# A conditioned transformer block on one core: the feed-forward's square sums made one slot earlier and turned behind x in the gate's bank

## The chip, the cores and the metric

The kernel runs on one core of one Trainium2 chip. The metric is device time in microseconds (us) of one execution. The kernel before takes 960.4 us, the median of three runs (960.19 to 960.7).

The engines named below: PE is TensorE (matrix products and transposes into PSUM), DVE is VectorE, ACT is ScalarE, POOL is GpSimd, and SP (SyncE) issues the transfers. Each engine executes its own list of instructions in order, and lists meet only through semaphores.

## The reference, cut to what matters

The input is 128 sequences of 64 tokens of 256 features, with one condition vector of 64 numbers for each sequence. All is float32.

```
x = layernorm(x) * weight + bias + tanh(cond @ lin_w.T + lin_b);  x = x * weight + bias
x = x + a_alpha * attention(a_gamma * rms(x) + a_beta)          # 16 heads of 16, softmax over 64 keys
x = x + f_alpha * ((silu(h @ gate_w.T) * (h @ hidden_w.T)) @ out_w.T + out_b),  h = f_gamma * rms(x) + f_beta
rms(x) = x / sqrt(mean(x * x over the 256 features) + 1e-6)
```

The gammas, betas and alphas are products of the condition with small matrices, one vector of 256 per sequence. The hidden width is 1024.

## The kernel before, in words

**Parts, slots, groups.** The 8192 tokens are worked in 32 parts of 256 tokens (four sequences). Features lie on the partitions and tokens along them, in two halves (KT = 2). One loop over slots `s`, from -8 to 141, is written out on every engine with the same conditions. A slot holds one sequence's attention (two, in every second slot) and one step of the feed-forward, whose four steps for a part fill one group of four slots. With `grp, j = s // 4, s % 4`, a group does at the same time: the first normalisation of part `grp + 2`, the keys, queries and values of part `grp + 1`, scores and softmax of part `grp`, attention's output of part `grp - 1` (at j = 3), the second normalisation of part `grp - 2`, and the feed-forward steps (gate, hidden, down) of part `grp - 3`. Below, "first slot" is j = 0 and "fourth slot" j = 3.

**Precision.** Each float32 product is made in three passes over rounded operands of type fp32r: an operand is split into `_hi` and `_lo` (ACT rounds to `_hi`, DVE or POOL subtracts to make `_lo`), and `three_pass` multiplies hi by hi, hi by lo and lo by hi (L361 to L363). Such a product, with 256 columns, is the bulk of what PE does.

**The second normalisation of part m = grp - 2.** Attention's output lies in bank 7 (`work`); DVE multiplies it by alpha (`gate_attention`, L777, writes `gated_a`), POOL adds it to the residual (`add_attention`, L1275), both in the fourth slot of the group before. In the first slot ACT squares the residual (`square_f`, L990) and POOL adds the two halves (`sum_squares_f`, L1223). In the second slot PE turns the 128x256 sums into PSUM in two transposes (`turn_squares`, L408), so that DVE can add over the features along a row (`mean_squares_out`, L785 and L788); POOL raises the result to -1/2 (`inverse_rms`, L1203). In the third slot PE spreads the inverse back over the partitions (`spread_inverses`, L415), DVE scales by it (L791), POOL adds beta; in the fourth, ACT and DVE split (`split_hi_f` L1002, `ffn_split_lo` L812, which writes `xf_lo`). The feed-forward of that part begins in the first slot of the next group.

**PSUM banks around this.** The gate's products go to bank 0, the hidden ones to bank 1, the output's to bank 2. Bank 1 is also `norm_bank`: in it x is turned (`turn_x`, L396, first slot), the square sums are turned (second slot) and the inverses are spread (third slot), each between two uses of it by `hidden`. So `turn_squares` waits in the second slot for `prod_made` of the step before. Bank 0 is also where the probabilities of every odd sequence are turned (L521), to be copied out by ACT (`probs_out`, L1055) before the gate's products of the same slot are begun. ACT takes tanh of the gate's bank (L1070), DVE multiplies it with the same bank (`activate`, L819) and with the hidden bank (`product`, L827), ACT rounds (L1076), DVE subtracts (`product_lo`, L833).

**DVE's list in a first slot**: `product_lo` of the step before (L833), a tiny instruction on token statistics (L716), the two minima of this slot's scores (`find_least`, L743, one for each of two sequences), and then the softmax's sums. For parts from 6 on, DVE also shifts the tokens of x, one tile of 128 at a time (`shift_tokens`, L703 and L707, writes `xin`), or takes their statistics (L669, then the small merges from L676). In the slot ahead of an even group a tile is shifted; in the slot ahead of an odd group the statistics are merged.

## Time and profile before

| | |
|---|---|
| median of 3 runs | 960.4 us (960.19 to 960.7) |
| profiled execution | 959.94 us, of which the span of instructions 958.1 us |
| granted TensorE clock | 0.999 |
| PE busy | 919.5 us, 96% of the span |
| DVE busy | 740.5 us, 77% |
| ACT busy | 634.9 us, 66% |
| POOL busy | 501.0 us, 52% |

The profile gives, for one execution, each engine's busy time, the time at which each instruction starts and how long it takes, and what an engine waited for. Two records of one engine that follow each other overlap a little: on DVE the next one starts some 0.08 us before the last one's end, and PE starts a new 256-column product every 0.12 us though its record is 0.28 us long. So a row's start time is what to compare with another row's start time.

### The profile page before, as it was taken

The page shows a single profiled execution, that of the slowest core. Times are in us where ns is not written, and L with a number is a line of the kernel's source. Part 1 is how long each engine was busy: PE and PEld are TensorE (multiplying, and loading weights), DVE is VectorE, ACT ScalarE, POOL GpSimd, SP SyncE. Part 2 cuts the span into 40 slices and gives each one's busy share as a digit, 9 for nine tenths or more (in the row PEclk, how much of TensorE's full clock was granted, in tenths as well). Part 3 has the DMA queues.
Part 4 walks back from the last instruction along what each step waited for, and adds up shares of the span by engine and source line. Part 5 has one row for each costly group of instructions (what it writes and reads, how often), then busy time and mean ns, then how long its engine had stood idle before and what let it go on. Part 6 is the DMA issues. An engine that isn't in the chain of part 4 may idle for free.

```text
span 958.1 us, 28583 instructions
## 1 busy us (share of the span) xinstructions
PE 919.5 (96%) x11064; PEld 883.9 (92%) x11064; DVE 740.5 (77%) x1433; ACT 634.9 (66%) x1837; POOL 501.0 (52%) x479
## 2 busy tenths in 40 slices
PE   5667999999999999999999999999999999999997
PEld 4557999999999999999999999999999999998997
DVE  5977788788778778877877887887788787667654
ACT  3656766767776776777677677767667766766432
POOL 4686455465655555555455555545555555453320
PEclk9999999999999999999999999999999999999999
DMA  6200011120020212002121210202110110100000
GB/s 224 75 2 29 13 24 56 25 51 22 10 57 24 57 24 51 13 18 57 23 57 24 49 12 20 58 24 56 25 36 23 24 36 18 18 13 13 13 12 24
DMA packets 40631, 33.77 MB, mean 35 GB/s; under 512 B 10800, under 2 KB 39984, under 8 KB 40496
## 3 DMA queue, kind: packets, MB, share of 16 engines
q1 hardware_dynamic: 40496, 31.93, 13.3%
q8 instruction: 89, 1.46, 0.7%
q14 instruction: 46, 0.38, 0.3%
HBM read 23.37 MB, written 8.55 MB: 33 GB/s over the span
## 4 chain that ended last, share of the span: by engine, by line
PE 89%; DVE 5%; issue 3%; POOL 2%; ACT 1%; DMA 0%; SPq 0%; DVEq 0%; ACTq 0%; POOLq 0%
PE psum L361 18%; PE psum L363 18%; PE psum L362 18%; PE psum L587 6%; PE psum L589 6%; PE psum L588 6%; PE psum L521 5%; PE psum L495 4%; PE psum L537 4%; PE psum L396 2%; PE psum L415 1%; DVE least L743 1%; PE psum L408 1%; POOL probs L1270 0%; DVE row_sum L759 0%
## 5 line engine op out<-in xcount | busy, mean ns | idle before, releaser
L361 PE MATMUL psum<-xf_hi,ffn_hi 128*128 128x256 f32 x1024 | 291.3, 284 | 2.1 <-ACT probsT L1055 1.6
L362 PE MATMUL psum<-xf_lo,ffn_hi 128*128 128x256 f32 x1024 | 288.1, 281 | 0.0
L363 PE MATMUL psum<-xf_hi,ffn_lo 128*128 128x256 f32 x1024 | 287.8, 281 | 0.0
L1047 ACT ACTIVATE probs<-psum,least 128x64 f32<-128x64 f32 x928 | 204.5, 354 | 38.5 <-DVE least L743 37.7
L1270 POOL TENSOR_TENSOR probs<-probs,inv_sum 128x512 f32<-128x512 f32 x128 | 133.9, 1047 | 154.1 <-DVE inv_sum L764 154.0
L361 PEld LDWEIGHTS psum<-xf_hi,ffn_hi 128*128 128x128 f32 x1024 | 192.7, 188 | 3.2 <-issue 2.7
L362 PEld LDWEIGHTS psum<-xf_lo,ffn_hi 128*128 128x128 f32 x1024 | 192.8, 188 | 0.0
L363 PEld LDWEIGHTS psum<-xf_hi,ffn_lo 128*128 128x128 f32 x1024 | 192.8, 188 | 0.0
L1076 ACT ACTIVATE prod_hi<-late 128x512 fp32r<-128x512 f32 x128 | 83.3, 651 | 127.6 <-DVE late L827 127.5
L587 PE MATMUL psum<-prod_hi,ffn_hi 128*128 128x256 f32 x512 | 144.1, 281 | 0.9 <-DVE prod_lo L833 0.9
L589 PE MATMUL psum<-prod_hi,ffn_lo 128*128 128x256 f32 x512 | 144.1, 282 | 0.0
L588 PE MATMUL psum<-prod_lo,ffn_hi 128*128 128x256 f32 x512 | 144.1, 281 | 0.0
L759 DVE TENSOR_REDUCE row_sum<-probs 128x8 f32<-128x512 f32 x128 | 87.0, 680 | 71.6 <-ACT probs L1047 71.6
L819 DVE SCALAR_TENSOR_TENSOR late<-tanh,psum 128x512 f32<-128x512 f32 x128 | 87.2, 681 | 64.6 <-ACT tanh L1070 63.4
L1070 ACT ACTIVATE tanh<-psum 128x512 f32<-128x512 f32 x128 | 78.3, 612 | 49.0 <-PE psum L363 46.6
L833 DVE TENSOR_TENSOR prod_lo<-late,prod_hi 128x512 fp32r<-128x512 f32 x128 | 93.4, 730 | 20.4 <-ACT prod_hi L1076 20.2
L1055 ACT ACTIVATE probsT<-psum 128x512 f32<-128x512 f32 x128 | 69.4, 594 | 54.9 <-PE psum L537 54.9
L587 PEld LDWEIGHTS psum<-prod_hi,ffn_hi 128*128 128x128 f32 x512 | 96.4, 188 | 1.1 <-issue 1.1
L1256 POOL TENSOR_TENSOR normed_f<-normed_f,mod 128x512 f32<-128x512 f32 x32 | 33.4, 1043 | 120.7 <-DVE normed_f L791 120.7
L589 PEld LDWEIGHTS psum<-prod_hi,ffn_lo 128*128 128x128 f32 x512 | 96.4, 188 | 0.0
L588 PEld LDWEIGHTS psum<-prod_lo,ffn_hi 128*128 128x128 f32 x512 | 96.4, 188 | 0.0
L743 DVE TENSOR_REDUCE least<-psum 128x8 f32<-128x512 f32 x128 | 82.7, 684 | 16.2 <-PE psum L495 16.2
(116 smaller groups left out, 2154.4 us busy)
## 6 DMA issues: line engine op xcount, KB each, us to landing
out_t_dram<-x_res SPq DMA_DIRECT2D x31, 256.0 KB, 3.0
xin<-x_dram SPq DMA_DIRECT2D x15, 512.0 KB, 6.7
shift_tok<-shift_rows SPq DMA_DIRECT2D x104, 64.0 KB, 3.1
inv_row<-inv_rows SPq DMA_DIRECT2D x26, 128.0 KB, 4.8
w_raw<-attn_w_dram SPq DMA_DIRECT2D x1, 1024.0 KB, 6.7
x_res<-gate_w_dram SPq DMA_DIRECT2D x1, 1024.0 KB, 9.4
late<-hidden_w_dram SPq DMA_DIRECT2D x1, 1024.0 KB, 11.3
w_raw<-out_w_dram SPq DMA_DIRECT2D x1, 1024.0 KB, 6.4
```

The source lines that it names most:

```text
L361: pe.matmul(out, stat_hi, mov_hi, start=first, stop=False)
L362: pe.matmul(out, stat_hi, mov_lo, start=False, stop=False)
L363: return pe.matmul(out, stat_lo, mov_hi, start=False, stop=last)
L587: pe.matmul(out, ffn_hi[:, 2, cols], hi, start=q == 0 and mt == 0 and u == 0, stop=False)
L588: pe.matmul(out, ffn_hi[:, 2, cols], prod_lo[f % 2][:, tok], start=False, stop=False)
L589: mm = pe.matmul(out, ffn_lo[:, 2, cols], hi, start=False, stop=q == 3 and mt == KT - 1 and u == 1)
L743: dve.tensor_reduce(least[g % 2][:].rearrange("p (r a) -> p r a", r=4), scores[g % 2], AX_X, ALU.min).then_inc(least_made, 1)
L759: dve.tensor_reduce(row_sum[g % 2][:], probs[g % 4][:].rearrange("p (h k) -> p h k", k=SEQ), AX_X, ALU.add).then_inc(sum_made, 1)
L819: dve.scalar_tensor_tensor(out=act_gate, in0=tanh[:], scalar=1.0, in1=gate_bank, op0=ALU.add, op1=ALU.mult).then_inc(act_made, 1)
L833: dve.tensor_tensor(prod_lo[f % 2][:], prod, prod_hi[f % 2][:].bitcast(F32), ALU.subtract).then_inc(prod_lo_made, 1)
L1047: op = act.activation(probs[g % 4][:, h * SEQ:(h + 1) * SEQ], scores[g % 2][:, h // 2, h % 2], ACT.Exp, bias=least[g % 2][:, h:h + 1], sca ...
L1270: pool.tensor_tensor(by_head, by_head, inv_sum[g % 2][:].unsqueeze(2).broadcast_to([P, 8, SEQ]), ALU.mult).then_inc(probs_made, 1)
```

## The change

Three things are done, for parts 2 to 31 (`sums_ahead`).

1. Attention's output is added first in the fourth slot: DVE's `gate_attention` moves ahead of `product_lo`, and POOL's `add_attention` moves ahead of `normalise_probs` (multiplying the probabilities) and `split_lo_a` (`xn_lo`).
2. The square sums are made in that same fourth slot: ACT squares after its tanh, ahead of rounding the product, and POOL adds the halves last in the slot.
3. The sums are turned in the next first slot, right behind x's four transposes, and into the gate's bank instead of bank 1. For this PE waits until the gate's bank has been read by `activate` and by the copy of the probabilities. DVE reads the sums right after the two minima, and the first gate product of the group waits until they are read (`ms_read`). In the second slot nothing of it is left.

No instruction is added or taken away.

```
+        def sums_ahead(m):
+            return 2 <= m < NPART
+
+        def square_bank(grp):
+            return gate_bank if sums_ahead(grp - 2) else norm_bank
...
             def gate(f):
...
+                if f % PSEQ == 0 and sums_ahead((f + FFN_AT) // PSEQ - 2):
+                    pe.wait_ge(ms_read, (f + FFN_AT) // PSEQ + 3)
...
         # PE's list
                     norm_bank_free(s)
                     if j == 0 and is_part(grp + 2):
                         turn_x(grp + 2)
+                if j == 0 and sums_ahead(grp - 2):
+                    pe.wait_ge(act_made, min(f, FFN_STEPS))
+                    if is_seq(s - 1):
+                        pe.wait_ge(probsT_out, s)
+                    turn_squares(grp)
...
-                if j == 1 and is_group(grp) and s >= 0:
+                if j == 1 and is_group(grp) and s >= 0 and not sums_ahead(grp - 2):
                     norm_bank_free(s)
                     turn_squares(grp)
...
         # DVE's list
-                if j == 1 and is_group(grp):
+                if j == 1 and is_group(grp) and not sums_ahead(grp - 2):
                     mean_squares_out(grp)
+                if j == 3 and sums_ahead(grp - 1):
+                    gate_attention(grp - 1)
                 if is_step(f - 1):
                     product_lo(f - 1)
...
+                if j == 0 and sums_ahead(grp - 2):
+                    mean_squares_out(grp)
...
         # ACT's list
-                if j == 0 and is_part(grp - 2) and s > FFN_AT:
-                    square_f(grp - 2)
...
                 if is_step(f):
                     half_tanh(f)
+                if j == 3 and sums_ahead(grp - 1):
+                    square_f(grp - 1)
...
         # POOL's list
+                if j == 3 and sums_ahead(grp - 1):
+                    add_attention(grp - 1)
                 if is_seq(s) and not wide(s):
                     normalise_probs(s)
...
-                if j == 3 and is_part(grp - 1):
+                if j == 3 and is_part(grp - 1) and not sums_ahead(grp - 1):
                     add_attention(grp - 1)
+                if j == 3 and sums_ahead(grp - 1):
+                    sum_squares_f(grp - 1)
```

The lists show it. In all of them the line numbers of the changed kernel are a few higher than those of the kernel before for the same code, and what stands in brackets are the semaphores that the instruction waits for.

PE, before, in a first slot, from the scores to the keys:

```order
L495 MATMUL psum<-k_heads,q_heads 64x128 x15
L396 MATMUL psum<-ident,xin 128x128 [waits y_tok,prod_made]
L396 MATMUL psum<-ident,xin 128x128 x3
L361 MATMUL psum<-xn_hi,w_hi 128x256 [waits gated_a_made,lo_a,probsT_out]
L362 MATMUL psum<-xn_lo,w_hi 128x256
```

PE, changed, at the same place (`xf_hi` begins the gate's products, after twelve of the keys, of which the rows between are left out):

```order
L501 MATMUL psum<-k_heads,q_heads 64x128 x15
L402 MATMUL psum<-ident,xin 128x128 [waits y_tok,prod_made]
L402 MATMUL psum<-ident,xin 128x128 x3
L414 MATMUL psum<-ident,square_sum_f 128x128 [waits sq_sum_f,probsT_out,act_made]
L414 MATMUL psum<-ident,square_sum_f 128x128
L367 MATMUL psum<-xn_hi,w_hi 128x256 [waits gated_a_made,lo_a,probsT_out]
...
L367 MATMUL psum<-xf_hi,ffn_hi 128x256 [waits ms_read,probsT_out,act_made,lo_f]
```

The two transposes of the sums now stand between x and the keys, and the gate's first product has `ms_read` as a further wait.

DVE, before, from the fourth slot of an odd group into the first slot of the next one:

```order
L833 TENSOR_TENSOR prod_lo<-late,prod_hi 128x512 [waits out_mm,prod_hi_made]
...
L777 TENSOR_TENSOR gated_a<-psum,mod 128x512 [waits resid_made,wo_mm]
L819 SCALAR_TENSOR_TENSOR late<-tanh,psum 128x512 [waits prod_made,tanh_made]
...
L812 TENSOR_TENSOR xf_lo<-normed_f,xf_hi 128x512 [waits hi_f]
L703 SCALAR_TENSOR_TENSOR xin<-xin,mean,rows 128x256
L707 SCALAR_TENSOR_TENSOR xin<-xin,rstd,shift_tok 128x256 [waits shift_loaded0,centred]
L833 TENSOR_TENSOR prod_lo<-late,prod_hi 128x512 [waits out_mm,prod_hi_made]
L716 TENSOR_SCALAR token_inv<-token_ms 128x2 [waits inv_sent,sq_tok]
L743 TENSOR_REDUCE least<-psum 128x8 [waits scores_read,scored] x2
L759 TENSOR_REDUCE row_sum<-probs 128x8 [waits scores_read]
```

DVE, changed, at the same place:

```order
L790 TENSOR_TENSOR gated_a<-psum,mod 128x512 [waits resid_made,wo_mm]
L846 TENSOR_TENSOR prod_lo<-late,prod_hi 128x512 [waits out_mm,prod_hi_made]
...
L825 TENSOR_TENSOR xf_lo<-normed_f,xf_hi 128x512 [waits hi_f]
L716 SCALAR_TENSOR_TENSOR xin<-xin,mean,rows 128x256
L720 SCALAR_TENSOR_TENSOR xin<-xin,rstd,shift_tok 128x256 [waits shift_loaded0,centred]
L846 TENSOR_TENSOR prod_lo<-late,prod_hi 128x512 [waits out_mm,prod_hi_made]
L729 TENSOR_SCALAR token_inv<-token_ms 128x2 [waits inv_sent,sq_tok]
L756 TENSOR_REDUCE least<-psum 128x8 [waits scores_read,scored] x2
L798 TENSOR_REDUCE square_mean<-psum 128x2 [waits inv_spread,ms_mm]
L801 TENSOR_SCALAR mean_sq<-square_mean 128x2 [waits ms_read]
L772 TENSOR_REDUCE row_sum<-probs 128x8 [waits scores_read]
```

(`xf_lo` is the lower half of the feed-forward's input, `xin` the tile of x that is being shifted.) `gated_a` has moved ahead of `prod_lo`, and the sums (`square_mean`, `mean_sq`) now follow the two minima.

POOL, before, over the same stretch:

```order
L1270 TENSOR_TENSOR probs<-probs,inv_sum 128x512 [waits inv_sum_made] x2
L1243 TENSOR_TENSOR xn_lo<-normed_a,xn_hi 128x512 [waits hi_a]
L1275 TENSOR_TENSOR x_res<-x_res,gated_a 128x2x256 [waits gated_a_made]
L1210 TENSOR_TENSOR token_inv<-token_inv,minus_half 128x2 [waits token_ms_out]
L1223 TENSOR_TENSOR square_sum_f<-squares_f 128x256 [waits ms_mm,squared_f]
L1251 TENSOR_TENSOR normed_f<-x_res,mod 128x512 [waits lo_f,resid_made]
```

POOL, changed:

```order
L1287 TENSOR_TENSOR probs<-probs,inv_sum 128x512 [waits inv_sum_made]
L1292 TENSOR_TENSOR x_res<-x_res,gated_a 128x2x256 [waits gated_a_made]
L1287 TENSOR_TENSOR probs<-probs,inv_sum 128x512 [waits inv_sum_made]
L1260 TENSOR_TENSOR xn_lo<-normed_a,xn_hi 128x512 [waits hi_a]
L1240 TENSOR_TENSOR square_sum_f<-squares_f 128x256 [waits ms_mm,squared_f]
L1227 TENSOR_TENSOR token_inv<-token_inv,minus_half 128x2 [waits token_ms_out]
L1268 TENSOR_TENSOR normed_f<-x_res,mod 128x512 [waits lo_f,resid_made]
```

The addition to `x_res` now comes first and the square sums last of the fourth slot, with the product of the probabilities and `xn_lo` between them.

## Rows read from the trace of the kernel before

**Rows 1.** Windows, steady stretch: window, length, busy us per engine, clock, DMA, GB/s.
```profile
120.00:840.00 720.00, 720.00 (x8800) 697.29 (x8799) 574.27 (x1103) 508.37 (x1529) 391.08 (x370) 1.00 0.15 33
```

**Rows 2.** Timeline of PE, probabilities turned in an even group's first slot: start us, us.
```profile
503.25 1.03 PE L521 MATMUL psum<-ident,probs 128*128 128x128 f32 x8
```

**Rows 3.** Timeline of PE, first slot of an even group, from the scores on.
```profile
504.80 0.69 PE L495 MATMUL psum<-k_heads,q_heads 32*64 32x128 f32 x32
505.42 0.66 PE L396 MATMUL psum<-ident,xin 128*128 128x128 f32 x4
505.84 0.37 PE L361 MATMUL psum<-xn_hi,w_hi 128*128 128x256 f32 x1
...
507.35 0.28 PE L361 MATMUL psum<-xf_hi,ffn_hi 128*128 128x256 f32 x1
```

**Rows 4.** Timeline of DVE, fourth slot into that first slot.
```profile
499.64 0.69 DVE L833 TENSOR_TENSOR prod_lo<-late,prod_hi 128x512 fp32r<-128x512 f32 x1
...
501.08 0.65 DVE L777 TENSOR_TENSOR gated_a<-psum,mod 128x512 f32<-128x512 f32 x1
...
502.55 0.69 DVE L827 TENSOR_TENSOR late<-psum,late 128x512 f32<-128x512 f32 x1
503.15 0.93 DVE L812 TENSOR_TENSOR xf_lo<-normed_f,xf_hi 128x512 fp32r<-128x512 f32 x1
504.00 1.50 DVE L703 SCALAR_TENSOR_TENSOR xin<-xin,mean,rows 128x256 f32<-128x256 f32 x1
...
506.61 1.28 DVE L743 TENSOR_REDUCE least<-psum 128x8 f32<-128x512 f32 x2
```

**Rows 5.** Timeline of POOL, the same stretch.
```profile
501.25 1.04 POOL L1270 TENSOR_TENSOR probs<-probs,inv_sum 128x512 f32<-128x512 f32 x1 [3.85 <-DVE inv_sum L764]
502.25 1.28 POOL L1243 TENSOR_TENSOR xn_lo<-normed_a,xn_hi 128x512 fp32r<-128x512 f32 x1
503.50 1.72 POOL L1275 TENSOR_TENSOR x_res<-x_res,gated_a 128x512 f32<-128x512 f32 x1
...
507.46 0.73 POOL L1223 TENSOR_TENSOR square_sum_f<-squares_f 128x256 f32<-128x256 f32 x1
```

**Rows 6.** Timeline of ACT, the copies of the probabilities there.
```profile
504.77 1.09 ACT L1055 ACTIVATE probsT<-psum 128x512 f32<-128x512 f32 x2 [0.87 <-PE psum L537]
```

**Rows 7.** Timeline of DVE, the sums' read in the second slot.
```profile
513.79 0.41 DVE L785 TENSOR_REDUCE square_mean<-psum 128x2 f32<-128x256 f32 x1
```

**Rows 8.** Timeline of PE, the last products of the span.
```profile
952.50 0.36 PE L587 MATMUL psum<-prod_hi,ffn_hi 128*128 128x256 f32 x1 [0.90 <-DVE prod_lo L833]
```

**Rows 9.** Timeline of DVE, what releases them.
```profile
951.66 0.69 DVE L833 TENSOR_TENSOR prod_lo<-late,prod_hi 128x512 fp32r<-128x512 f32 x1 [0.70 <-ACT prod_hi L1076]
```

**Rows 10.** Timeline of DVE, first slot of an odd group.
```profile
534.57 1.28 DVE L743 TENSOR_REDUCE least<-psum 128x8 f32<-128x512 f32 x2
```

**Rows 11.** Timeline of PE, the gate's first product there.
```profile
535.47 0.28 PE L361 MATMUL psum<-xf_hi,ffn_hi 128*128 128x256 f32 x1
```

**Rows 12.** Timeline of PE, second slot: the sums' transposes and what follows.
```profile
513.04 0.38 PE L408 MATMUL psum<-ident,square_sum_f 128*128 128x128 f32 x2
513.18 0.37 PE L361 MATMUL psum<-xf_hi,ffn_hi 128*128 128x256 f32 x1
513.38 0.28 PE L362 MATMUL psum<-xf_lo,ffn_hi 128*128 128x256 f32 x1
```

**Rows 13.** Timeline of DVE, first slot of group 4.
```profile
113.06 1.28 DVE L743 TENSOR_REDUCE least<-psum 128x8 f32<-128x512 f32 x2
```

**Rows 14.** Timeline of PE, the gate's first product there.
```profile
112.81 0.28 PE L361 MATMUL psum<-xf_hi,ffn_hi 128*128 128x256 f32 x1
```

**Rows 15.** Timeline of DVE, first slot of group 31.
```profile
870.57 1.29 DVE L743 TENSOR_REDUCE least<-psum 128x8 f32<-128x512 f32 x2 [1.01 <-PE psum L495]
```

**Rows 16.** Timeline of PE, gate's first products, groups 31 and 32; bracket: idle before.
```profile
870.97 0.36 PE L361 MATMUL psum<-xf_hi,ffn_hi 128*128 128x256 f32 x1 [0.51 <-ACT probsT L1055]
...
896.21 0.36 PE L361 MATMUL psum<-xf_hi,ffn_hi 128*128 128x256 f32 x1 [1.13 <-ACT probsT L1055]
```

More of the change, by code:

```diff
@@ L403, in turn_squares @@
                     for i in range(2):
-                        mm = pe.transpose(norm_bank[:, i * P:(i + 1) * P], square_sum_a[:, i * P:(i + 1) * P], ident[:])
+                        mm = pe.transpose(square_bank(grp)[:, i * P:(i + 1) * P], square_sum_a[:, i * P:(i + 1) * P], ident[:])
                 if is_part(grp - 2):
@@ L407, in turn_squares @@
                     for i in range(2):
-                        mm = pe.transpose(norm_bank[:, (2 + i) * P:(3 + i) * P], square_sum_f[:, i * P:(i + 1) * P], ident[:])
+                        mm = pe.transpose(square_bank(grp)[:, (2 + i) * P:(3 + i) * P], square_sum_f[:, i * P:(i + 1) * P], ident[:])
                 mm.then_inc(ms_mm, 1)
@@ L784, in mean_squares_out @@
                 cols = norm_cols(grp, 1)
-                dve.tensor_reduce(square_mean[:, cols], norm_bank.rearrange("p (n c) -> p n c", c=P)[:, cols], AX_X, ALU.add
+                dve.tensor_reduce(square_mean[:, cols], square_bank(grp).rearrange("p (n c) -> p n c", c=P)[:, cols], AX_X, ALU.add
                                   ).then_inc(ms_read, 1)
@@ L1311, in _ @@
                 if j == 0 and is_part(grp - 2) and not wide(s):
-                    sum_squares_f(grp - 2)
+                    if not sums_ahead(grp - 2):
+                        sum_squares_f(grp - 2)
                     apply_gamma_f(grp - 2)
@@ L1331, in _ @@
                     split_lo_a(grp + 2)
-                if j == 3 and is_part(grp - 1):
+                if j == 3 and is_part(grp - 1) and not sums_ahead(grp - 1):
                     add_attention(grp - 1)
+                if j == 3 and sums_ahead(grp - 1):
+                    sum_squares_f(grp - 1)
                 if j == (grp == 1) and grp % 2 == 1 and 1 <= (grp + 3) // 2 < NBLK:
```

## The prediction

> **What bounds the kernel now.** I read the page's busy times first, where PE is far ahead of the others. Then the windows: over the 720 us from 120 to 840 PE is busy for all 720.00, at full clock (column 1.00), and DVE for 574 [rows 1]. Whatever PE idles lies at the two ends. So in the steady stretch nothing that another engine saves can pay; only PE's own list can become shorter, and any new wait on it comes out in full. The question is therefore what the change makes PE wait for. For that I read the timelines of the four engines around one first slot, and ask for each of the waits added to PE when its releaser would be ready. The steady groups are alike in two kinds, even (a tile of x is shifted in the slot ahead) and odd (statistics are merged there); one of each is read.
>
> **PE's list.** In the second slot the two transposes and their surroundings go. The transposes start at 513.04 and the second product behind them at 513.38, 0.34 us, where a product alone takes 0.12; so PE saves 0.22 us for each group [rows 12]. In the first slot x's four transposes take 505.84 - 505.42 = 0.42 us, 0.105 each [rows 3]; two more in the same chain cost 0.21. By itself the move is worth nothing: the same two transposes, elsewhere.
>
> **The new waits in front of the transposes** are three. `act_made` lies before `prod_made`, which x's transposes wait for already: nothing. `probsT_out`: the second copy ends at 504.77 + 1.09 = 505.86 [rows 6], while x's transposes are through at 505.84 [rows 3]: about 0.15 late. The sums come from POOL: below, they are ready at 505.5. So this first wait costs 0.0 to 0.2, and it is not added, because a later one covers it.
>
> **The wait in front of the gate.** The gate's products overwrite the bank, so PE now needs `ms_read`. Behind x and the sums stand only the keys' twelve products, 507.35 - 505.84 = 1.5 us [rows 3]. DVE reads the sums only after both minima. Their price from the minima's start: the pair takes 1.28, less the 0.08 by which records overlap [rows 4], the read 0.41 [rows 7], and from DVE's last write to PE's start 0.15 (951.66 + 0.69 = 952.35, PE at 952.50 [rows 8, 9]). Sum: 1.76 us. If DVE met the scores at once, some 0.1 after their end at 504.80 + 0.69 = 505.49 [rows 3], PE would be let go at 507.35, before the 507.56 at which it arrives with two more transposes. But DVE is late there: it begins the minima at 506.61 [rows 4], 1.1 us after the scores. In the odd group it begins at 534.57 [rows 10] and the gate stands at 535.47 [rows 11]. In the kernel before nobody minds, as the gate needs nothing of the minima; after it, everything that makes DVE late in the first slot stands on PE's path.
>
> **Is DVE later or earlier than before?** Its work ahead of the minima is the same: `gated_a` only changes places with `prod_lo` and the softmax's sum. What can differ are the blocks between DVE and POOL. The trace shows them: `xin` (L703) takes 1.50 us at 504.00 while POOL's addition runs from 503.50 to 505.22, and it ends 0.28 after that; `xf_lo` takes 0.93 at 503.15 and ends 0.55 after POOL's `xn_lo` (502.25 + 1.28 = 503.53); the addition takes 1.72 and ends 1.14 after `xf_lo` [rows 4, 5]. They take turns. I lay the new order on these rows, for the even group. `gated_a` takes the place at 499.64 (0.65, to 500.29), `prod_lo` starts at 500.21 and ends at 500.90; POOL's addition, released at the same moment, ends 1.14 later, 502.04. The probabilities take 1.0 (501.25 to 502.25 in the rows), then `xn_lo` runs 503.04 to 504.33, just where `xf_lo` wants to start (503.15, since DVE's chain up to the product at 502.55 is as long as before). `xf_lo` ends at 504.33 + 0.55 = 504.88, not 504.08. POOL's sums take 0.54 less than the addition unhindered (0.73 against `xn_lo`'s like-sized 1.28), so end at 504.88 + 0.60 = 505.48; `xin` ends 0.28 later, 505.76, not 504.00 + 1.50 = 505.50. The minima start at 506.61 + 0.26 = 506.87. So the addition's block leaves the stretch, but `xn_lo` and the sums have moved into it. For the odd group the same reckoning (a longer block of `xf_lo`, a shorter one of the merges) gives no shift that I trust; I take none.
>
> The Trainium skill, "GPSIMD Engine Reference", section "Key points", says that GpSimd shares its SBUF interfaces with VectorE and contends with DVE instructions that have two SBUF inputs. The slow rows above are all of that kind, so the trace agrees. Were there no such block between `xn_lo` and `xf_lo`, the even group would keep its 506.61 and the sum below would be 3.1 us smaller.
>
> **The sum.**
> - Even steady group: PE is let go at 506.87 + 1.76 = 508.63 in place of 507.35: 1.28, less the 0.22 of the second slot, 1.06.
> - Odd steady group: 534.57 + 1.76 = 536.33 in place of 535.47: 0.86 - 0.22 = 0.64.
> - Groups 5 to 28, twelve of each: 12 x 1.70 = 20.4.
> - Group 4: 113.06 + 1.76 = 114.82 against 112.81 [rows 13, 14]: 2.0 - 0.2 = 1.8.
> - Groups 29 and 30: no tile of x is shifted any more; taken as nothing.
> - Group 31 has no keys to hide behind: 870.57 + 1.76 = 872.33 against 870.97 [rows 15, 16]: 1.36 - 0.22 = 1.1.
> - Groups 32 and 33, without scores: PE waits for the copies (896.21 [rows 16]), then two transposes (0.38), the read (0.41) and the way back (0.15 and as much to DVE), less 0.22: 0.8 each, 1.6.
>
> Together 24.9 us. The profiled execution took 959.94, so 984.8; it lies 0.5 under the median of the runs, so I say 985. PE's stalls are near 1 us each; its first product is as long after 1.13 us of idleness as after 0.51 (0.36 both [rows 16]), so I take no loss of clock.
>
> The bounds of the one term that matters, the lateness: with DVE meeting the scores, the steady groups cost nothing, and the ends 2 to 3, 962.5. With POOL's `xn_lo` and sums both held in front of DVE's whole chain (1.28 + 0.73 = 2.0 of block where the rows of before have 0.3 + 1.0), even groups cost some 0.6 more and odd ones as much: 985 + 14 = 999. I choose the middle, as it is laid on rows.
>
> **Queues that the moved steps pass.** ACT's square of 0.6 us now stands between tanh and rounding the product; its input is ready at 502.04, the product at 503.2, so it is done by 502.8 and delays nothing. In the first slot ACT loses it, which brings nothing, since ACT waits for the minima there. POOL's probabilities are done at 503.1 instead of 502.3; PE turns the slot's eight pieces from 503.25 on, and this sequence's are the last four, so from about 503.7 [rows 2]: still in time, by 0.6. If the addition were slower by that much, PE would wait there too. SP issues nothing that moves.
>
> **Rivals.**
> 1. *The blocks are gone.* With the addition early, DVE comes to the first slot with 1 us less of block (that of L703 [rows 4]), starts the minima at about 505.6, and the gate is released in time. For it: the addition was the one that blocked L703. Against it: `xn_lo` and the sums now run there. It gives 960 to 963; with the sums' turn off the second slot at the end of the span, at best no change.
> 2. *Faster.* PE's list is 0.22 shorter in the second slot, and at the end the waits on `prod_made` ahead of the transposes go. If the two transposes in the first slot ran behind the four at less than 0.105 each, and DVE were in time, 30 x 0.1 and 1 us of the end would be won: 956. The rows show 0.105 for each of four, so little speaks for it.
> 3. *Much slower: the sums themselves are late.* POOL's chain in the fourth slot is addition, probabilities, `xn_lo`, sums. If each block costs it another 0.5, the sums end at 506.5, past PE's arrival at 505.84; PE then stands before the keys, which no longer hide anything, and the read follows 0.5 after. Each steady group costs 1.7 to 2: about 1000. It decides from 505.9 on; my chain ends at 505.48, only 0.4 short.
> 4. *Slower, but less:* the odd groups' lateness shrinks (product 0.3 earlier, no merge block), and half the sum is left: 972.
>
> **How the numbers follow.** The forecast, 985 with 976 to 993 as its own range: 0.57. Rival 4, 964 to 976: 0.16. Rival 3: 0.08. Rival 1: 0.12, of which 0.07 within 0.2% of before (958.5 to 962.3, about what a measurement of this kernel can tell from no change), 0.03 above it, 0.02 below. Rival 2: 0.03. The rest, 0.04, is slower in some other way. Range: from 962 to 994, which takes in the upper part of rival 1 and leaves out the rest of it, rival 2 and most of rival 3. Faster 0.05, same 0.07, slower 0.88.
>
> **What would show it.** In the profile after: PE's waits show the gate's first product of every fourth slot held by DVE's `square_mean`, some 28 times and near 1 us each, more in even groups than in odd ones; PE is no longer 720 of 720 busy in the middle; the second slot has no transposes of sums; `xf_lo` is longer than 0.93 in even groups and L703 shorter than 1.50. It is wrong if the minima start within 0.4 us of the scores' end (rival 1), or if the transposes of the sums, and not the gate, are what waits (rival 3).

## The result: 993.0 us, slower by 3.3%

The changed kernel takes 993.0 us, the median of four runs (989.9 to 993.45), against 960.31 for the kernel before; the ratio is 1.0333, with a 95% interval from 1.0311 to 1.0354. The profiled execution took 992.7 us with a span of 990.8, so 32.7 us more than the span before.

In the window of the steady stretch PE is no longer busy throughout, as it was in [rows 1], but for 704.14 of 720 us; the columns are those of that group:

```profile
120.00:840.00 720.00, 704.14 (x8501) 676.42 (x8503) 555.14 (x1072) 499.86 (x1484) 378.20 (x359) 1.00 0.15 32
```

In the steady stretch it waits for one thing. The list of PE's waits over the whole span (us in total, times, longest us) is led by a line that did not exist before:

```profile
PE psum L367 <- DVE square_mean L798: 20.0, 28, 1.4
```

Now the same first slot of an even group as in [rows 3], some 15.5 us later in this trace. PE's timeline: scores, x's four transposes, the two of the sums, the keys, and the gate's first product, with its idle time in brackets.

```profile
520.34 0.69 PE L501 MATMUL psum<-k_heads,q_heads 32*64 32x128 f32 x32
520.97 0.66 PE L402 MATMUL psum<-ident,xin 128*128 128x128 f32 x4
521.50 0.41 PE L414 MATMUL psum<-ident,square_sum_f 128*128 128x128 f32 x2
521.67 0.36 PE L367 MATMUL psum<-xn_hi,w_hi 128*128 128x256 f32 x1
...
524.25 0.36 PE L367 MATMUL psum<-xf_hi,ffn_hi 128*128 128x256 f32 x1 [0.92 <-DVE square_mean L798]
```

The keys begin at 521.67 and the gate could begin 1.5 us later; it begins at 524.25. DVE's timeline shows why, in the place of [rows 4]:

```profile
515.19 0.68 DVE L790 TENSOR_TENSOR gated_a<-psum,mod 128x512 f32<-128x512 f32 x1
515.79 0.68 DVE L846 TENSOR_TENSOR prod_lo<-late,prod_hi 128x512 fp32r<-128x512 f32 x1
...
518.10 0.69 DVE L840 TENSOR_TENSOR late<-psum,late 128x512 f32<-128x512 f32 x1
518.71 1.70 DVE L825 TENSOR_TENSOR xf_lo<-normed_f,xf_hi 128x512 fp32r<-128x512 f32 x1
520.33 0.95 DVE L716 SCALAR_TENSOR_TENSOR xin<-xin,mean,rows 128x256 f32<-128x256 f32 x1
...
522.39 1.28 DVE L756 TENSOR_REDUCE least<-psum 128x8 f32<-128x512 f32 x2
523.58 0.41 DVE L798 TENSOR_REDUCE square_mean<-psum 128x2 f32<-128x256 f32 x1
```

The minima (L756) start at 522.39, 1.36 us after the scores' end (520.34 + 0.69 = 521.03), where they started 1.1 after it before. The read of the sums (L798) ends at 523.99, and PE starts at 524.25. And POOL's timeline, to be held against [rows 5]:

```profile
515.95 1.67 POOL L1292 TENSOR_TENSOR x_res<-x_res,gated_a 128x512 f32<-128x512 f32 x1 [3.00 <-DVE gated_a L790]
517.58 1.04 POOL L1287 TENSOR_TENSOR probs<-probs,inv_sum 128x512 f32<-128x512 f32 x1
518.58 1.28 POOL L1260 TENSOR_TENSOR xn_lo<-normed_a,xn_hi 128x512 fp32r<-128x512 f32 x1
519.82 1.18 POOL L1240 TENSOR_TENSOR square_sum_f<-squares_f 128x256 f32<-128x256 f32 x1
```

`xf_lo` (L825) wants to start at 518.71, just after `xn_lo` (L1260) has, and takes 1.70 us; POOL's sums (L1240) then take 1.18 in place of 0.73, as they wait for `xf_lo`, and the shift of x (L716) takes 0.95. The odd groups wait less; here is the gate's first product of the next one, to be held against [rows 11]:

```profile
553.05 0.36 PE L367 MATMUL psum<-xf_hi,ffn_hi 128*128 128x256 f32 x1 [0.40 <-DVE square_mean L798]
```

To see how the 32.7 us are spread, compare the starts of the scores in the two traces, first of group 4 and then of group 29. Before:

```profile
110.26 0.47 PE L495 MATMUL psum<-k_heads,q_heads 32*64 32x128 f32 x16
...
813.93 0.58 PE L495 MATMUL psum<-k_heads,q_heads 32*64 32x128 f32 x24
```

After:

```profile
112.54 0.47 PE L501 MATMUL psum<-k_heads,q_heads 32*64 32x128 f32 x16
...
840.50 0.67 PE L501 MATMUL psum<-k_heads,q_heads 32*64 32x128 f32 x28
```

Group 4's scores are 2.28 us later, though nothing but the additions and sums of the slot ahead of them is moved before that; group 29's are 26.57 later; the end is 32.7 later. So the 25 groups in between cost 24.3, the start 2.3 and the last stage 6.1. Of the latter, half is a matter of clock, as the section on the prediction works out. Two windows of the last stage, in which the column before the last two is the granted clock, read:

```profile
900.00:905.00 5.00, 5.00 (x31) 5.00 (x31) 2.24 (x4) 3.07 (x14) 1.71 (x2) 0.66 0.01 3
925.00:930.00 5.00, 3.68 (x19) 3.50 (x20) 0.75 (x3) 0.95 (x2) 0.71 (x1) 0.73 0.00 0
```

The clock is 0.66 and 0.73 there, a mean of the levels 2.4 and 1.2 GHz. It falls behind PE's waits in groups 31 and 32; these are the two of group 32:

```profile
925.61 0.41 PE L414 MATMUL psum<-ident,square_sum_f 128*128 128x128 f32 x2 [1.24 <-ACT probsT L1072]
926.73 0.36 PE L367 MATMUL psum<-xf_hi,ffn_hi 128*128 128x256 f32 x1 [0.71 <-DVE square_mean L798]
```

### The profile page after: what moved, and what is told of

Its sections match the earlier page's. It is cut to its first block, busy times and chain, and to the rows that moved or that the text cites. A ratio compares the mean times of both kernels' runs of the same rounds, so it can differ in the third digit from the quotient of the medians.

```text
span 990.8 us, 28612 instructions
## 1 busy us (share of the span) xinstructions
PE 933.8 (94%) x11064; PEld 891.6 (90%) x11064; DVE 738.4 (75%) x1433; ACT 643.4 (65%) x1837; POOL 502.4 (51%) x479
## 4 chain that ended last, share of the span: by engine, by line
PE 52%; DVE 18%; DMA 8%; issue 8%; ACT 7%; POOL 5%; SPq 0%; DVEq 0%; ACTq 0%; POOLq 0%
PE psum L367 12%; PE psum L369 11%; PE psum L368 11%; DMA inv_rows<-token_inv 5%; DVE least L756 4%; PE psum L595 4%; PE psum L596 4%; PE psum L597 4%; DMA inv_row<-inv_rows 3%; DVE xf_lo L825 3%; PE psum L527 2%; ACT probs L1064 2%; DVE xin L716 2%; DVE late L832 2%; PE psum L543 2%
## 5 line engine op out<-in xcount | busy, mean ns | idle before, releaser
L756 DVE TENSOR_REDUCE least<-psum 128x8 f32<-128x512 f32 x128 | 82.6, 683 | 39.4 <-PE psum L501 39.3
L840 DVE TENSOR_TENSOR late<-psum,late 128x512 f32<-128x512 f32 x128 | 88.5, 691 | 12.8 <-PE psum L369 10.1
L846 DVE TENSOR_TENSOR prod_lo<-late,prod_hi 128x512 fp32r<-128x512 f32 x128 | 88.9, 695 | 11.5 <-ACT prod_hi L1093 11.4
```

Of the source, the lines that this page charges most:

```text
L756: dve.tensor_reduce(least[g % 2][:].rearrange("p (r a) -> p r a", r=4), scores[g % 2], AX_X, ALU.min).then_inc(least_made, 1)
L840: dve.tensor_tensor(prod, hidden_bank, act_gate, ALU.mult).then_inc(prod_made, 1)
L846: dve.tensor_tensor(prod_lo[f % 2][:], prod, prod_hi[f % 2][:].bitcast(F32), ALU.subtract).then_inc(prod_lo_made, 1)
```

## The experiments

All are compared with the kernel before on the same chip in the same session, where it took 961.4, 961.5 and 961.2 us; it varies more there than in the first session (959.5 to 962.7, 959.8 to 965.0 and 959.5 to 963.8 in the three), and the section on what was not expected says what goes with it.

**The early addition alone.** The kernel before with this edit (the two calls that it replaces, later in the lists, are skipped where `early` is true):

```
 # DVE
+                early = j == 3 and 2 <= grp - 1 < NPART
+                if early:
+                    gate_attention(grp - 1)
                 if is_step(f - 1):
                     product_lo(f - 1)
 # POOL
+                if early:
+                    add_attention(grp - 1)
                 if is_seq(s) and not wide(s):
                     normalise_probs(s)
```

> The kernel before with one part of the change alone: in the fourth slot, for parts 2 to 31, gate_attention stands ahead of product_lo on DVE and the addition ahead of the probabilities and xn_lo on POOL. Squares, sums and their turn stay where they were. My theory (what costs is PE's wait for the sums' read in front of the gate, nothing else in the steady stretch): PE waits for none of this, 960.3 us, within 1. Rival A (the early addition disturbs DVE and POOL so much that PE feels it, through late probabilities or a late xf_lo): half a us for each group, 970 to 975.

Measured: 960.47 us, ratio 0.9989 (0.9980 to 0.9999). In the window PE is busy as before:

```profile
120.00:840.00 720.00, 719.87 (x8800) 697.58 (x8800) 573.24 (x1106) 510.76 (x1532) 390.56 (x370) 1.00 0.16 33
```

So rival A falls. Whether the 0.1% was a gain was measured again with eleven runs:

> The kernel with the early addition alone, once more, in five rounds: it was 0.9989 of the kernel before with an interval that ends at 0.9999. My theory: PE's steady stretch is full with it as without, so no measurable difference, a ratio from 0.9985 to 1.0005. Rival (it saves 0.02 us in each group, as its profile's scores drift from 1.3 to 0.6 us behind those of before over 16 groups): 0.9975 to 0.999, a gain clear of noise.

Measured: 961.73 us, ratio 0.9999 (0.9987 to 1.0011). No difference that can be measured. The drift that I had read from one pair of profiles (0.6 us over the steady groups) is not in the profile of this second measurement.

**The early sums, turned where they were.** The changed kernel with these edits, and the same on DVE's side:

```
         def square_bank(grp):
-            return gate_bank if sums_ahead(grp - 2) else norm_bank
+            return norm_bank
...
-                if f % PSEQ == 0 and sums_ahead((f + FFN_AT) // PSEQ - 2):
-                    pe.wait_ge(ms_read, (f + FFN_AT) // PSEQ + 3)
...
-                if j == 0 and sums_ahead(grp - 2):
-                    pe.wait_ge(act_made, min(f, FFN_STEPS))
-                    if is_seq(s - 1):
-                        pe.wait_ge(probsT_out, s)
-                    turn_squares(grp)
...
-                if j == 1 and is_group(grp) and s >= 0 and not sums_ahead(grp - 2):
+                if j == 1 and is_group(grp) and s >= 0:
```

> The changed kernel with the addition, the squares and the sums early in the fourth slot as it has them, but turned in the second slot in bank 1 as before, and read by DVE there, so that the gate's first product waits for nothing new. My theory: 960 us, within 1, since the whole loss comes with the turn in the first slot. Rival A (the early sums lengthen the blocks between DVE and POOL and this is what costs): the larger part of the 33 us stays, 975 to 990.

Measured: 966.21 us, ratio 1.0050 (1.0034 to 1.0067). That is outside the 960 plus or minus 1 of my theory, but the rival's 975 is farther off: 28 of the 33 us leave with the turn. Of the rest, the scores of group 4 are 2.6 us late in this profile, which is the start again, and 2.8 us come up in the steady stretch. They are no line of the waits; they are short. In the third slot of an even group PE turns the probabilities and goes on to the values (L543); start times of this kernel:

```profile
521.60 1.21 PE L527 MATMUL psum<-ident,probs 128*128 128x128 f32 x8
522.74 0.65 PE L543 MATMUL psum<-probsT,v_diag 128*32 128x64 f32 x32
```

From the one to the other it takes 1.14 us, where a turn of eight that waits for nothing takes 0.97. POOL makes the last of these probabilities until 522.09, just when PE is through with the first four pieces, and POOL had waited for DVE's sum:

```profile
521.05 1.04 POOL L1278 TENSOR_TENSOR probs<-probs,inv_sum 128x512 f32<-128x512 f32 x1 [1.28 <-DVE inv_sum L770]
```

So it is DVE that is late. The early addition is not the reason, since the kernel with the early addition alone takes 0.97 there. What is added here is the early squares and sums. POOL's sums now hold the shift of x. In the kernel with the addition alone it takes 0.47 us:

```profile
505.34 0.47 DVE L703 SCALAR_TENSOR_TENSOR xin<-xin,mean,rows 128x256 f32<-128x256 f32 x1
```

In this one it takes 0.95:

```profile
508.77 0.95 DVE L709 SCALAR_TENSOR_TENSOR xin<-xin,mean,rows 128x256 f32<-128x256 f32 x1
```

With it the minima start 1.37 us after the scores' end, and 0.89 after it with the addition alone (1.12 in the kernel before). These waits are about 1.9 of the 2.8 us (11 even groups, 0.17 each); the rest was not taken apart.

**The read ahead of the minima.** The changed kernel with one step moved on DVE:

```
+                if j == 0 and sums_ahead(grp - 2):
+                    mean_squares_out(grp)
                 if s % 2 == 0:
                     for g in (s, s + 1):
                         if is_seq(g):
                             find_least(g)
...
-                if j == 0 and sums_ahead(grp - 2):
-                    mean_squares_out(grp)
```

> The changed kernel with one edit: in the first slot DVE reads the turned sums ahead of the two minima, not behind them. My theory: the read then starts as soon as the sums are turned, about 0.5 us after the transposes' start, and PE is released before it has done the keys' twelve products; the 0.91 and 0.40 us of the steady groups go (12 of each, and 1.37 in group 4: 17 us), and what stays is the two transposes with their wait for the probabilities' copy in each group (0.2 to 0.3 net, 24 groups: 6 us), the end of the span (6 us, as groups 32 and 33 have no minima to be moved) and the start: 975 to 976. Rival B (the loss lies in PE's own list, two transposes of another kind in front of the keys, and the wait on DVE only shows it): little changes, above 987. Rival C (the minima, now up to 0.5 us later, delay the exponentials and so the probabilities, and PE waits for these in place of the gate): a new wait on L527 and a time of 985 or more.

Measured: 972.27 us, ratio 1.0096 (1.0060 to 1.0132). The waits go, and PE is as full as ever in the steady stretch:

```profile
120.00:840.00 720.00, 719.99 (x8769) 693.25 (x8769) 574.75 (x1097) 510.63 (x1528) 386.99 (x367) 1.00 0.15 33
```

Its list of PE's waits has three of 28 left, all at the end:

```profile
PE psum L367 <- DVE square_mean L798: 2.5, 3, 1.1
```
In the steady stretch 20.8 us leave (24.3 become 3.5 by the starts of the scores): about 21 us for moving one instruction of 0.41 us past two of 0.6. The runs spread widely, 966.25 to 972.47 us; the three slow ones have a mean clock of 0.989, the other 0.999. Rival B falls, as PE's list is the same. Rival C falls in its size: no line on the probabilities comes up in the list of waits, but in the even groups' third slot PE takes 1.08 to 1.19 us over the turn in place of 0.97, as in the kernel with the old turn.

**The read between the minima**, by the same step inside the loop.

```
                             find_least(g)
+                            if g == s and j == 0 and sums_ahead(grp - 2):
+                                mean_squares_out(grp)
...
-                if j == 0 and sums_ahead(grp - 2):
+                if j == 0 and sums_ahead(grp - 2) and not is_seq(s):
                     mean_squares_out(grp)
```

> The changed kernel with the sums' read between the two minima of the first slot, so one minimum (0.6 us) earlier than in the changed kernel. My theory (PE's release follows the read one to one): the waits of the even steady groups shrink from 0.91 to about 0.3, those of the odd ones from 0.40 to nothing, in group 4 from 1.37 to 0.8. With 12 of each kind 12.6 us less than the changed kernel: 993 - 12.6 = 980, and between it and the kernel that reads first (972). Rival (what counts is only whether the read stands ahead of or behind some other event, such as the copies of the probabilities): the same as one of the two, 972 or 993.

Measured: 978.21 us, ratio 1.0180 (1.0152 to 1.0209). The list of waits has halved its count, since the odd groups dropped out of it:

```profile
PE psum L367 <- DVE square_mean L798: 7.5, 16, 1.1
```

PE's timeline, the gate's first product in an even group's first slot:

```profile
516.43 0.36 PE L367 MATMUL psum<-xf_hi,ffn_hi 128*128 128x256 f32 x1 [0.33 <-DVE square_mean L798]
```

It waits for 0.33 us. 0.91 less 0.60 is 0.31: PE's release follows the read one to one.

**Without the last three parts.** The changed kernel with a shorter range, and ACT's squares of those parts back in the first slot:

```
         def sums_ahead(m):
-            return 2 <= m < NPART
+            return 2 <= m < NPART - 3
...
+                if j == 0 and is_part(grp - 2) and s > FFN_AT and not sums_ahead(grp - 2):
+                    square_f(grp - 2)
```

> The changed kernel with the new order for parts 2 to 28 only; parts 29 to 31, whose sums are turned in groups 31 to 33 after the last full groups, are done as before. My theory: the end of the span costs 6 us in the changed kernel (scores of group 31 lie 27.2 us later than before, the end 32.7 later), of which some 3.4 are two stretches at a granted clock of half after PE's waits there: 987, and a granted clock without the low stretches at 900 to 905 and 925 to 930. Rival D (the end is late for what came before it, not for its own waits): 992 to 993.

Measured: 986.70 us, ratio 1.0264 (1.0249 to 1.0280): 6.3 less than the changed kernel. In the profiles the last stage costs 0.3 us over the kernel before, where it cost 6.1. The windows of the end are back at full clock:

```profile
900.00:905.00 5.00, 4.53 (x39) 4.33 (x39) 4.86 (x12) 3.04 (x11) 2.36 (x3) 1.00 0.00 0
925.00:930.00 5.00, 5.00 (x44) 5.00 (x44) 3.70 (x9) 1.23 (x2) 1.70 (x2) 1.00 0.00 2
```

**Both edits together**, the read first and the last parts as before:

> The changed kernel with both edits, the read ahead of the minima and parts 29 to 31 done as before. My theory: both costs are gone and they add up, so what stays over the kernel before is PE's own surplus in the first slot, 0.15 us for each of 24 groups as the kernel with the read first showed, 3.6 us: 965, with no wait of PE on the read. Rival (the costs overlap, the end's waits come only with the stalls ahead): the end brings nothing more and it stays at 970 or above.

Measured: 965.60 us, ratio 1.0038 (1.0019 to 1.0056). The two costs add up and the rival falls: PE does not wait for the read at all. In the profile of this kernel the start costs 2.4 us, the steady stretch 3.6 and the last stage 0.7. The remainder came out as expected in its size, but only in part for the reason given. In the even groups' third slot PE waits for the probabilities again, 1.17 us from the turn to the values in place of 0.97:

```profile
634.96 1.24 PE L527 MATMUL psum<-ident,probs 128*128 128x128 f32 x8
636.13 0.65 PE L543 MATMUL psum<-probsT,v_diag 128*32 128x64 f32 x32
```

Over 12 even groups these waits are some 2.2 of the 3.6 us, and PE's own surplus in the first slot is the smaller part. Still it is slower than before: no arrangement of the turn in the first slot that was tried wins anything.

**POOL's order.** The changed kernel with the last two steps of POOL's fourth slot exchanged:

```
-                if j == 3 and is_part(grp + 2) and s != -1 and not 0 <= s < FFN_AT:
-                    split_lo_a(grp + 2)
...
                 if j == 3 and sums_ahead(grp - 1):
                     sum_squares_f(grp - 1)
+                if j == 3 and is_part(grp + 2) and s != -1 and not 0 <= s < FFN_AT:
+                    split_lo_a(grp + 2)
```

> The changed kernel with POOL's last two steps of the fourth slot exchanged: the square sums ahead of xn_lo. My theory (POOL and DVE take turns, so only the sum of POOL's work in DVE's stretch counts, not its order): xf_lo is held for the sums (0.5 us) and not for xn_lo (1.0), and the shift of x is held for xn_lo instead; DVE starts the minima of even groups where it does now, 1.3 us after the scores' end, within 0.15, and the time stays within 2 us of 992. Rival (a block of xf_lo counts more than one of the shift): the minima start 0.4 earlier or later and the time moves by 5 us or more.

Measured, in one run: 992.9 us. DVE's timeline (`xf_lo`, the shift of x, the minima):

```profile
520.44 1.19 DVE L825 TENSOR_TENSOR xf_lo<-normed_f,xf_hi 128x512 fp32r<-128x512 f32 x1
521.54 1.50 DVE L716 SCALAR_TENSOR_TENSOR xin<-xin,mean,rows 128x256 f32<-128x256 f32 x1
...
524.15 1.28 DVE L756 TENSOR_REDUCE least<-psum 128x8 f32<-128x512 f32 x2
```

`xf_lo` takes 1.19 where it took 1.70, and the shift 1.50 where it took 0.95: 2.69 against 2.65 together, and the minima come 1.37 us after the scores' end, as before this edit (1.36). The block moves from one victim to the other, and its sum stays.

**The shift of x behind the minima.** The changed kernel with DVE's shift of the third tile in the next first slot:

```
-                if tile_at(s) is not None and tile_at(s) % TILES < 3:
+                if tile_at(s) is not None and tile_at(s) % TILES < 2:
                     shift_tokens(tile_at(s))
...
                 if j == 0 and sums_ahead(grp - 2):
                     mean_squares_out(grp)
+                if tile_at(s - 1) is not None and tile_at(s - 1) % TILES == 2:
+                    shift_tokens(tile_at(s - 1))
```

> The changed kernel with DVE's shift of the third tile of x (L716 and L720 in the changed kernel, 0.95 and 0.48 us) moved from the fourth slot of the odd groups to the next first slot, behind the minima and the read. My theory (DVE's lateness at the minima is what PE pays in even groups): the minima of even groups start about 1.3 us earlier, near 0.1 after the scores' end, and the wait of 0.91 goes in 12 groups, while the odd groups keep their 0.40: 993 - 11 = 982, with some 13 waits of PE on the read left in the steady stretch. Rival (the read itself is slow, or PE's release takes its time after the transposes of the sums, however early DVE is): 990 or more.

Measured: 991.37 us, ratio 1.0299 (1.0273 to 1.0324). By its time the rival is right; by its waits it is not. PE's wait on the read has gone from the even groups, as foreseen, and a new one stands in its place:

```profile
PE psum L367 <- DVE square_mean L798: 8.4, 16, 1.1
PE psum L367 <- ACT x_res L1003: 6.1, 13, 0.5
```

ACT's timeline shows where it is from: after the copies of the probabilities it has the square of the shifted tile next in its list (L994), sits idle for it, and only then copies x out of bank 1 (L1003), which the hidden products wait for.

```profile
525.21 0.42 ACT L994 ACTIVATE squares_a<-xin 128x256 f32<-128x256 f32 x1 [3.00 <-DVE xin L720]
...
525.63 0.58 ACT L1003 ACTIVATE x_res<-psum 128x512 f32<-128x512 f32 x1
```

I had moved an instruction past a reader without asking what stood behind that reader. So the theory was tried again with the square moved along:

```
-                if tile_at(s - 1) is not None:
+                if tile_at(s - 1) is not None and tile_at(s - 1) % TILES != 2:
                     square_tokens(tile_at(s - 1))
...                  # behind exponentials(s)
+                if tile_at(s - 1) is not None and tile_at(s - 1) % TILES == 2:
+                    square_tokens(tile_at(s - 1))
```

> The kernel with the third tile's shift behind the minima, and in addition ACT's square of that tile behind the exponentials of the same first slot; in the kernel with the shift alone behind, ACT stood before that square until DVE had shifted (3.00 us idle), and x's copy out of bank 1 (L1003) came late for PE's hidden products, 0.5 us in each even group. My theory (that new wait alone ate the gain of the earlier minima): PE waits neither for x's copy nor, in even groups, for the read; the even groups cost 0.3 in place of 1.3 us, 12 of them: 991.4 - 12 = 979 to 981. Rival (the even groups' cost is in PE's list and moves to whatever is last): 988 or more.

Measured: 979.90 us, ratio 1.0190 (1.0169 to 1.0211).

```profile
PE psum L367 <- DVE square_mean L798: 7.8, 16, 1.1
```

Of 28 waits on the read 16 are left, the odd groups', group 4's and the end's, and 11.5 us are won over the kernel with the shift alone (13.1 over the changed one). DVE's lateness at the minima was what the even groups paid for. (The minima of this kernel, and of the one before it, start 0.5 after the scores' end and not 0.1, since `product_lo` is now the one that waits for POOL's sums. It was enough.)

## Why the prediction was right, and where its size was off

**The mechanism** is the forecast's: PE's gate held by DVE's read, in groups 4 to 28 and 31 to 33, more in even ones than in odd ones. The profile has the 28 waits, and the experiments take them away or shorten them in three ways (the read first, between, DVE earlier). The size came out 8 us over the 985, at the upper edge of the range (994): the start added 2.3, the steady groups 3.0 and the end 3.4 to what was reckoned, and group 4 took 0.9 off.

**The lateness.** The reckoning laid on the rows of before holds to 0.02 us. With the 15.54 us between the traces taken off, `xf_lo` ends at 504.87 (reckoned 504.88), the sums at 505.46 (505.48), the shift of x at 505.74 (505.76), the minima start at 506.85 (506.87). The block between DVE and POOL, on which this rests, is shown by the exchange of POOL's steps, which moved it and kept its sum. In the odd group no shift was taken; there DVE is 0.12 nearer to the scores (0.84 for 0.96).

**The steady groups** cost 23.4 us and not 20.4: 1.2 for an even one (reckoned 1.06) and 0.74 for an odd one (0.64). Two terms were mis-sized. I took 0.15 us from DVE's last write to PE's start; here it is 524.25 - 523.99 = 0.26, and 0.25 to 0.26 in 22 of the 24 groups. And the product behind the wait is followed by the next one after 0.20 us, not after 0.12, which the sum left out; this is 0.08 in each group. In an even group the two make up the difference, to 0.05. In an odd group the longer way back is made good by DVE being 0.12 nearer, which was luck, and the 0.08 remains. Why the way back is longer here than in the row it was taken from was not settled; in group 33 it was 0.14.

**Group 4** cost 0.9, not 1.8. The kernel before had short waits of its own in the two slots behind, of which its timeline of PE names the one ahead of the sums' transposes:

```profile
119.31 0.30 PE L408 MATMUL psum<-ident,square_sum_f 128*128 128x128 f32 x1 [0.30 <-issue]
```

After the longer wait in the first slot they are gone.

**The end** was reckoned at 1.1 + 1.6 = 2.7 and cost 6.1. The step that failed is the sentence "so I take no loss of clock". I had read it off one product's length behind one wait. In the changed kernel the clock falls to its lower level behind the two waits of group 31 (0.62 and 0.95 us) and again behind those of group 32 (1.24 and 0.71 us); (1 - 0.66) x 5 = 1.7 us of full-speed time are missing in the first window above, and about as much around the second. The kernel without the last parts has neither, and its end costs 0.3 us.

But the waits do not bring the fall each time. The kernel with the read between the minima has the same two waits in group 32, and its clock is at 1.00 over the hundred us around them:

```profile
911.86 0.41 PE L414 MATMUL psum<-ident,square_sum_f 128*128 128x128 f32 x2 [1.24 <-ACT probsT L1074]
912.98 0.36 PE L367 MATMUL psum<-xf_hi,ffn_hi 128*128 128x256 f32 x1 [0.71 <-DVE square_mean L798]
```

```profile
870.00:970.00 100.00, 94.58 (x996) 91.31 (x994) 61.02 (x101) 43.25 (x106) 29.91 (x26) 1.00 0.04 15
```

The profiles of all kernels that keep the waits of the end can be sorted by the number of falls in the last stage (leaving out its last 5 us, where the clock is below 1.00 in the kernel before too). With no fall the stage costs 3.1 us over the kernel before (the read between, and the shift and square behind), with one fall 4.7 (the read first, POOL's order, the shift behind), and with two 6.1 (the changed kernel). So the waits were reckoned well, 2.7 for 3.1, and the other half of the 6.1 is the clock, which one execution loses and another does not. Why it falls in one and not in another was not settled.

**The start**, 2.3 us, is not the change's, as the next section shows. Sum: 2.3 + 0.9 + 23.4 + 6.1 = 32.7.

**The rivals.** Rival 1 (blocks gone) fell: the minima are later than before in even groups. Rival 2 fell: two transposes behind x's four cost 0.28 us with the wait for the probabilities' copy, and 0.22 are saved elsewhere. The best that was reached with the turn in the first slot is the 965.6 of the two edits together, and with the early sums turned where they were before it is 966.2. Rival 3 (the sums late) did not come: they end at 521.00, PE turns them at 521.50. It was near the right size all the same, for other reasons. Rival 4 fell with the odd groups' 0.40 us of idle PE each; their lateness did shrink, but only by 0.12 us. Among the moved steps the claim that POOL's late probabilities stay in time was true: the turn in the first slot takes 0.97 us. What the forecast did not look at are the probabilities of the third slot, which come late with DVE by 0.17 us in even groups where PE does not wait at the gate, as the kernel with the old turn shows. In the changed kernel this is hidden, and the turn takes 0.97 there too.

## What to carry to other kernels

Where one engine is full, ask of a change not what it does for the others but what it makes that engine wait for, and read the releaser's whole list up to that point: here an instruction of 0.41 us cost 21 us through what stood ahead of it. When a step moves past others on one engine, follow each of its readers to what stands behind them on their own engines. Waits near an end, where nothing else fills the engine, can cost twice their length if the clock falls behind them, and the same waits brought the fall in one execution and not in another.

## What the runs showed of the hardware that was not expected

**The same start takes a different time in each execution.** In the profile of the kernel before PE had its full clock all the way to 110 us; in that of the changed kernel, with the same lists there, it had not. Before:

```profile
30.00:40.00 10.00, 5.81 (x74) 5.28 (x74) 9.55 (x19) 7.58 (x15) 6.28 (x8) 1.00 0.04 13
80.00:90.00 10.00, 8.02 (x121) 7.42 (x120) 6.65 (x18) 8.44 (x26) 6.66 (x8) 1.00 0.20 67
```

After:

```profile
30.00:40.00 10.00, 6.56 (x69) 5.78 (x68) 8.19 (x19) 6.04 (x12) 6.77 (x7) 0.83 0.04 13
80.00:90.00 10.00, 8.81 (x116) 8.14 (x117) 4.42 (x14) 6.42 (x17) 5.80 (x7) 0.83 0.21 67
```

In this stage PE waits often in both, and whether its clock falls to the lower level varies between runs: over the first 110 us the granted clock is 1.00, 0.97, 0.98, 0.97 and 0.92 in the profiles of the kernel before, the changed one, the early addition, the early sums and the read first, and the scores of group 4 come 0, 2.3, 1.3, 2.6 and 4.1 us later. In the profiles of the read between the minima and of the kernel without the last parts, which have the changed kernel's lists up to there, they come only 1.0 us later, so the 2.3 us are not the change's. The kernel before itself reads 959.5 to 965.0 over the three sessions, and its three longest runs are those with the lowest mean clock (0.990 and 0.991); runs at 0.998 and more reach from 959.5 to 962.5, so the clock is not all of it. Why it falls in one execution and not in another at the same work was not settled. It puts an error of one to four us on any comparison of single profiles of such a kernel, and it can move a median of four: the read first has three runs at 972.2 to 972.5 and one at 966.25.

**DVE and POOL take turns, in full.** The forecast was built on this, and the runs bear it out. Where a DVE instruction with two operands in SBUF starts while a POOL instruction runs, it ends 0.3 to 0.6 us after that one, and the next POOL instruction ends late in its turn; in the even group the times could be added up from the rows to 0.04 us. The Trainium skill says in "GPSIMD Engine Reference", section "Key points", that GpSimd and VectorE contend where a DVE instruction has two SBUF inputs. The trace agrees, and adds the size: `xf_lo` takes 1.70 us in the even group read and 1.74 in the odd one, 1.0 more than the like-sized `prod_lo` (0.68), which starts before POOL does.
